# Recurrent layer of a fused four-layer kernel: row statistics on ScalarE, group scale and row mixing on GpSimd, single-term weights on TensorE

## The reference, cut to what matters

```
xa = ln(x) ; sx = shift(xa) - xa                      # shift: the row of the token before
xxx = tanh((xa + sx * maa_x) @ maa_w1)                # five low-rank rows
xm = xa + sx * (maa_stack + xxx @ maa_w2)             # five mixed inputs
w = exp(-exp(time_decay + tanh(xw @ td_w1) @ td_w2)) ; r, k, v = xr @ Wr.T, xk @ Wk.T, xv @ Wv.T
g = silu(xg @ Wg.T)
s = k v^T + w s ; out = r (u k v^T + s)               # a scan over 64 tokens, 32 heads of 8
og = (out - mean) / sqrt(var + 1e-5)                  # per head, 8 channels
x1 = x + (og * g) @ Wo.T
xc = ln(x1) ; sx2 = shift(xc) - xc
xk2 = xc + sx2 * ffn_maa_k ; xr2 = xc + sx2 * ffn_maa_r
out = x1 + sigmoid(xr2 @ Wfr.T) * (square(relu(xk2 @ Wfk.T)) @ Wfv.T)
```

## Time and profile before

| | us |
|---|---|
| median of 3 runs | 1036.51 (1035.86 to 1045.05) |
| the profiled execution, own time | 1037.27 |
| its span | 1035.4 |
| busy: PE | 946.3 (91%) |
| busy: DVE | 595.9 (58%) |
| busy: ACT | 431.0 (42%) |
| busy: POOL | 410.0 (40%) |

### The profile page before, as it was taken

The page is one execution under the profiler, slowest core; times in us unless marked ns, Lnnn a source line. Parts: engine busy times, 40 slices in busy tenths (PEclk is TensorE's granted clock), DMA queues, the critical chain, the costliest instruction groups (busy, mean ns, idle before and its releaser), DMA issues.

```text
span 1035.4 us, 21403 instructions
## 1 busy us (share of the span) xinstructions
PE 946.3 (91%) x8296; PEld 803.9 (78%) x8296; DVE 595.9 (58%) x1004; ACT 431.0 (42%) x910; POOL 410.0 (40%) x558
## 2 busy tenths in 40 slices
PE   6888887968989999999999999999996978999986
PEld 4667765856778888899887988888985877878854
DVE  5889993667644443334363444433357457988871
ACT  3566663237643333333343333333323223545542
POOL 2223253875366343333166432433317512333320
PEclk9999997999999999999998999999998998999997
DMA  9000000140011110111101111110100100000000
GB/s 307 11 2 1 3 1 11 42 150 1 2 52 47 51 51 24 47 36 51 47 19 54 37 51 46 51 51 21 41 16 22 41 1 1 1 6 7 6 12 15
DMA packets 24145, 37.12 MB, mean 36 GB/s; under 512 B 4432, under 2 KB 16528, under 8 KB 23824
## 3 DMA queue, kind: packets, MB, share of 16 engines
q1 hardware_dynamic: 24080, 36.23, 11.3%
HBM read 35.17 MB, written 1.05 MB: 35 GB/s over the span
## 4 chain that ended last, share of the span: by engine, by line
PE 76%; DVE 8%; ACT 7%; issue 4%; POOL 4%; DMA 1%; SPq 0%; ACTq 0%; POOLq 0%; DVEq 0%
PE ps L1193 16%; PE ps L722 11%; PE ps L1832 9%; PE ps L1210 9%; PE ps L1252 6%; PE ps L1228 3%; PE ps L811 3%; PE ps L394 2%; PE ps L345 2%; PE ps L1238 2%; PE ps L1983 1%; PE ps L1910 1%; PE ps L297 1%; ACT sb L1617 1%; PE ps L1871 1%
## 5 line engine op out<-in xcount | busy, mean ns | idle before, releaser
L772 POOL TENSOR_TENSOR sb<-sb 128x256 fp32r<-128x256 f32 (+1 forms) x128 | 95.5, 746 | 302.0 <-DMA sb<-in_heads_a 149.7
L1193 PE MATMUL ps<-sb 128*128 128x512 f32 x768 | 187.8, 396 | 1.0 <-issue 1.0
L1193 PEld LDWEIGHTS ps<-sb 128*128 128x128 f32 x768 | 139.6, 188 | 33.0 <-ACT sb L1318 3.2
L722 PE MATMUL ps<-sb 128*128 128x256 f32 x1152 | 148.7, 287 | 0.5 <-DVE sb L859 0.4
L722 PEld LDWEIGHTS ps<-sb 128*128 128x128 f32 x1152 | 142.5, 193 | 2.7 <-issue 0.8
L774 POOL TENSOR_TENSOR sb<-sb 128x256 fp32r<-128x256 f32 (+1 forms) x128 | 115.6, 903 | 10.0
L1832 PE MATMUL ps<-sb 128*128 128x128 f32 (+2 forms) x672 | 101.0, 309 | 12.4 <-ACT sb L2116 6.3
L1832 PEld LDWEIGHTS ps<-sb 128*128 128x128 f32 (+1 forms) x672 | 89.6, 202 | 21.8 <-issue 8.0
L1415 DVE SCALAR_TENSOR_TENSOR sb<-ps,sb 128x512 fp32r<-128x512 f32 x64 | 45.1, 747 | 97.5 <-ACT sb L1351 97.5
L1210 PE MATMUL ps<-sb 128*128 128x256 f32 x768 | 99.2, 285 | 0.4 <-DVE sb L1383 0.4
L1210 PEld LDWEIGHTS ps<-sb 128*128 128x128 f32 x768 | 95.0, 191 | 3.0 <-issue 0.9
(11 more groups left out here) (211 smaller groups left out, 1595.7 us busy)
## 6 DMA issues: line engine op xcount, KB each, us to landing
sb<-in_heads_a SPq DMA_DIRECT2D x32, 386.0 KB, 3.0
sb<-in_heads_c SPq DMA_DIRECT2D x16, 256.0 KB, 3.6
sb<-in_heads_b SPq DMA_DIRECT2D x32, 128.0 KB, 2.9
sb<-in_mlp_a SPq DMA_DIRECT2D x16, 128.5 KB, 2.1
sb<-in_mlp_b SPq DMA_DIRECT2D x16, 128.0 KB, 2.1
sb<-in_w_r SPq DMA_DIRECT2D x1, 2048.0 KB, 7.6
sb<-in_encT SPq DMA_DIRECT2D x1, 1024.0 KB, 5.9
sb<-in_ctx SPq DMA_DIRECT2D x1, 1024.0 KB, 8.3
```

The lines of the kernel that those rows point to most:

```text
L722: last = pe.matmul(m.acc(t), lhsT[x], rhs[w], start=opens and n == 0, stop=False, skip_group_check=True)
L772: pool.tensor_tensor(high, src, one, ALU.mult).then_inc(*G.did(name + "_high", u))
L1193: last = pe.matmul(m.ps[u][:, c, :], m.w_parts[u][w][:, (KD * q + k) * P:(KD * q + k + 1) * P], rows[x][:, k, c * 512:(c + 1) * 512], star ...
```

## The change

Five edits in the recurrent layer. (1) The statistics of both row norms leave DVE: ACT runs an Identity with a sum, a Copy that makes the negative mean, and a Square with a sum; POOL makes the variance, the power and the product of the two (three instructions where there were two). (2) DVE forms xa + sx * maa_x itself (`lora_rows`, two instructions per tile), and `lora` has one term. (3) POOL forms xk2 and xr2 (`ffn_rows`, five instructions on 128x256 per tile), and `ffn1` has one term. (4) The root and the reciprocal of the group norm go from ACT and DVE to POOL: one scale-and-add and one power of -0.5, both on 128x32. (5) The scaling of weights is gone except for one. Two edits of order in the first layer: DVE does `stats` and `variance` of the next item after `keys` in place of before it, and POOL does `row_split` first in its slot; and at its end TensorE does `turn_rows` of the last tile between the two first pieces of the MLP, with ACT doing `mlp_rows` ahead of the two Gelus.

```diff
@@ attn0, last slot: TensorE, ACT, DVE, POOL
                 fc1(pe, ph, m, 4, u, 0, 0)
-        turn_rows(slot - 3)
+                if u == 0:
+                    turn_rows(slot - 3)
+        if slot < SLOTS - 1:
+            turn_rows(slot - 3)
...
         rows(slot)
+        mlp_rows(slot - 3)
         if slot == SLOTS - 1:
             for u in range(STREAMS):
                 gelu_rows(act, ph, m, ACT.Gelu_apprx_tanh, u, 0, 0)
-        mlp_rows(slot - 3)
...
-        if slot:
-            stats(slot + 1)
-            variance(slot + 1)
         keys(slot)
         if slot == 0:
             vec.wait_ge(m.s_x[1], 16)
-            stats(1)
-            variance(1)
+        stats(slot + 1)
+        variance(slot + 1)
@@ rwkv_tensor
-                           [(m.maa_w1[:, k, cols], xa[:, k, :, 1:S + 1]) for k in range(KD)]
-                           + [(m.maa_w1s[:, k, cols], xa[:, k, :, 0:S]) for k in range(KD)])
+                           [(m.maa_w1[:, k, cols], m.xl[i % 2][:, k, :]) for k in range(KD)])
...
+            product(m.c1[:, e * P:(e + 1) * P], [(m.wr[:, W_FK, k, e * P:(e + 1) * P], m.xk[:, k, :]) for k in range(KD)])
+        product(m.c1[:, D:2 * D], [(m.xr[:, k, :], m.wr[:, W_FR, k, :]) for k in range(KD)])\
+            .then_inc(*done["kk_rr"].did(i))
@@ rwkv_scalar
+    def stats(i, tag, at, dst):
+        a, own = i % 2, m.own_act
+        total, squares, mean = m.mv[a][:, at, 0:1], m.mv[a][:, at, 1:2], m.rstd[a][:, at:at + 1]
+        if i >= 2:
+            act.wait_ge(*done[tag + "_turned"].at(i - 2))
+        act.activation(dst[a][:, :], m.x[:, i, :], ACT.Identity, accum_out=total).then_inc(*own.did(tag + "_sum", i))
+        act.wait_ge(*own.at(tag + "_sum", i))
+        act.activation(mean, total, ACT.Copy, scale=-1.0 / D).then_inc(*own.did(tag + "_mean", i))
+        act.wait_ge(*own.at(tag + "_mean", i))
+        act.activation(dst[a][:, :], m.x[:, i, :], ACT.Square, bias=mean, accum_out=squares)\
+            .then_inc(*done[tag + "_eps"].did(i))
...
         ffn_rows(slot - 5)
+        f_stats(slot - 4)
+        a_stats(slot + 1)
         rows(slot)
...
         square(slot - 3)
-        std(slot - 3)
@@ rwkv_vector
+    def lora_rows(i):
+        vec.wait_ge(*m.own_vec.at("sx", i))
...
+            last = vec.scalar_tensor_tensor(out=split(m.xl[i % 2][:, k, :]), in0=split(m.sx[i % 2][:, k * P:(k + 1) * P]),
+                                            scalar=m.col("maa_x", k), in1=m.xa[i % 2][:, k, :, 1:S + 1], op0=ALU.mult,
+                                            op1=ALU.add)
+        last.then_inc(*m.own_vec.did("xl", i))
@@ rwkv_gpsimd
+    def ffn_rows(i):
+        own, wide = m.own_pool, lambda name: bc(m.cols(name), 2, [P, KD, P])
+        tokens = lambda s: m.xc[:, :, :, s:s + S].rearrange("p k b s -> p (k b) s")
+        split = lambda x: x.rearrange("p k (b s) -> p (k b) s", b=2)
+        pool.wait_ge(*own.at("f_state", i))
+        pool.wait_ge(*done["xc"].at(i))
+        pool.tensor_tensor(split(m.xd), tokens(0), tokens(1), ALU.subtract).then_inc(*own.did("xd", i))
+        pool.wait_ge(*own.at("xd", i))
+        pool.tensor_tensor(m.xk, m.xd, wide("ffn_k"), ALU.mult)
+        pool.tensor_tensor(m.xr, m.xd, wide("ffn_r"), ALU.mult).then_inc(*own.did("xkr", i))
+        pool.wait_ge(*own.at("xkr", i))
+        pool.tensor_tensor(split(m.xk), split(m.xk), tokens(1), ALU.add)
+        pool.tensor_tensor(split(m.xr), split(m.xr), tokens(1), ALU.add).then_inc(*done["f_state"].did(i))
...
+    def group_rstd(i):
+        n = D // HS
+        pool.wait_ge(*done["gsum"].at(i))
+        pool.tensor_scalar(m.sm[0][:, :], m.sm[0][:, :], 1.0 / HS, EPS, ALU.mult, ALU.add)\
+            .then_inc(*m.own_pool.did("group_var", i))
+        pool.wait_ge(*m.own_pool.at("group_var", i))
+        if i >= 1:
+            pool.wait_ge(*done["normed"].at(i - 1))
+        pool.tensor_tensor(m.rc[0][:, :], m.sm[0][:, :], m.col("pow").to_broadcast([P, n]), ALU.pow)\
+            .then_inc(*done["gstd"].did(i))
...
     for slot in range(TILE_SLOTS):
+        f_state(slot - 7)
+        ffn_rows(slot - 7)
         f_rstd(slot - 6)
         a_state(slot - 2)
-        a_rstd(slot)
+        a_rstd(slot - 1)
         first(slot - 4)
+        group_rstd(slot - 5)
         receive(slot - 4)
-        f_state(slot - 6)
         gated(slot - 5)
         bonus(slot - 3)
```

More of the change, by code:

```diff
@@ L702, in attn0_gpsimd @@
             rstd(0)
+        row_split(slot - 4)
         row_rstd(slot - 3)
@@ L1973, in ffn1 @@
     def ffn1(i):
-        pe.wait_ge(*done["xc"].at(i))
         pe.wait_ge(*done["f_state"].at(i))
-        parts = [(m.wr[:, W_FK, :, :], m.wr[:, W_FR, :, :], k, 1) for k in range(KD)]\
-            + [(m.wfks, m.wfrs, k, 0) for k in range(KD)]
         for e in range(KD):
[L1979 to L1982, removed]
-                last = pe.matmul(m.c1[b * S:(b + 1) * S, D:2 * D], m.xc[:, k, b, s:s + S], wr[:, k, :], start=n == 0,
-                                 stop=n == len(parts) - 1)
-        last.then_inc(*done["kk_rr"].did(i))
+            product(m.c1[:, e * P:(e + 1) * P], [(m.wr[:, W_FK, k, e * P:(e + 1) * P], m.xk[:, k, :]) for k in range(KD)])
+        product(m.c1[:, D:2 * D], [(m.xr[:, k, :], m.wr[:, W_FR, k, :]) for k in range(KD)])\
+            .then_inc(*done["kk_rr"].did(i))
     @of_tile
@@ L2079, in std @@
     @of_tile
-    def std(i):
-        act.wait_ge(*done["gsum"].at(i))
-        act.activation(m.sm[0][:, :], m.sm[0][:, :], ACT.Sqrt, bias=m.col("eps"), scale=1.0 / HS)\
-            .then_inc(*done["gstd"].did(i))
-    @of_tile
     def heads(i):
@@ L2194, in shift @@
             .then_inc(*m.own_vec.did("sx", i))
+    @of_tile
+    def lora_rows(i):
+        vec.wait_ge(*m.own_vec.at("sx", i))
+        if i >= 2:
+            vec.wait_ge(*done["lora"].at(i - 2))
+        for k in range(KD):
+            split = lambda x: x.rearrange("p (b s) -> p b s", b=2)
+            last = vec.scalar_tensor_tensor(out=split(m.xl[i % 2][:, k, :]), in0=split(m.sx[i % 2][:, k * P:(k + 1) * P]),
+                                            scalar=m.col("maa_x", k), in1=m.xa[i % 2][:, k, :, 1:S + 1], op0=ALU.mult,
+                                            op1=ALU.add)
+        last.then_inc(*m.own_vec.did("xl", i))
     @of_tile
@@ L2277, in group_sum @@
         vec.wait_ge(*done["square"].at(i))
+        if i >= 1:
+            vec.wait_ge(*done["gstd"].at(i - 1))
         vec.tensor_reduce(m.sm[0][:, :], m.sq[:, :].rearrange("p (h j) -> p h j", j=HS), AX, ALU.add)\
             .then_inc(*done["gsum"].did(i))
[L2281 to L2284 removed]
     @of_tile
@@ L2323, in rwkv_vector @@
         products0(slot - 5)
-        f_variance(slot - 7)
         bonus(slot - 6)
@@ L2330, in rwkv_vector @@
         shift(slot - 3)
+        lora_rows(slot - 3)
         scan0(slot - 5)
-        group_rstd(slot - 6)
         group_norm(slot - 6)
@@ L2342, in rwkv_vector @@
         attended(slot - 6)
-        a_variance(slot)
-        f_stats(slot - 6)
         close(slot - 8)
@@ L2352, in rstd @@
     def rstd(i, tag, at):
+        a, own = i % 2, m.own_pool
+        var, squares, mean, scale = (m.mv[a][:, at, 0:1], m.mv[a][:, at, 1:2], m.rstd[a][:, at:at + 1],
+                                     m.rstd2[a][:, at:at + 1])
         pool.wait_ge(*done[tag + "_eps"].at(i))
-        norm_scales(pool, m, i % 2, at, (tag + "_pow", i), done[tag + "_rstd"].did(i))
+        pool.tensor_scalar(var, squares, 1.0 / D, EPS, ALU.mult, ALU.add).then_inc(*own.did(tag + "_var", i))
+        pool.wait_ge(*own.at(tag + "_var", i))
+        pool.tensor_tensor(scale, var, m.col("pow"), ALU.pow).then_inc(*own.did(tag + "_pow", i))
+        pool.wait_ge(*own.at(tag + "_pow", i))
+        pool.tensor_tensor(mean, mean, scale, ALU.mult).then_inc(*done[tag + "_rstd"].did(i))
     @of_tile
```

68 lines of the change are left out of this document (19 added, 49 removed).

## The result

The changed kernel takes 1071.03 us (median of 4 runs, 1068.21 to 1073.27) against 1037.92 (4 runs, 1035.86 to 1045.05): ratio 1.0305, 95% interval 1.0247 to 1.0363. The forecast was 1041, with a range to 1056; the change is 33 us slower. The profiled execution took 1072.52 us, its span is 1070.7.

What follows compares the result with a forecast made beforehand. The prediction saw TensorE setting the recurrent layer's pace, DVE close behind, and a loop of both bounding the first layer. 1037.3 + 11.7 (recurrent) - 7 (first layer) = 1042 profiled, so 1041 as median; 8-in-10 range 1022 to 1056.

Steps and rivals of the forecast that it cites:

- The line through three widths: Power on POOL: 550, 1034 and 1655 ns at 1, 4 and 8 columns, extended to 5.45 us at 32.
- DVE's wait: Recurrent layer's steady slots: DVE idles 3.2 us ahead of `group_norm` for POOL's power, which 2.7 us of work covers in part.
- rival (b): Power on POOL cheap at 32 columns, near a plain add's 0.73 us; TensorE sets 17.2 per slot; 1012; chance 0.12.
- -7 forecast: First layer: earlier `keys` save 5 us and the last tile's earlier rows 2.1; together -7, bounds 0 and -9.
- I take 20.5 per steady slot: Recurrent layer: a steady slot goes from 20.08 to 20.5 us, between 19.9 and 21.5.
- 0.6 for TensorE's clock behind it: Steady slots: after TensorE idles for `group_norm`, some 4 us at half speed push `mixes` about 0.6 us past DVE.
- the scans themselves do not seem to be stretched: DVE's scans in the recurrent layer: not lengthened by POOL's instructions, an argument against the shared-port rival of 1051.
- Rival (a): Slots 3 to 7: POOL's power takes the shared port, the second `lora_rows` waits; +10 us, 1051; with its like 0.30.
- My -3.5 for slots 0 to 2: Recurrent layer's first slots, without group norm: one-term `lora` and an earlier third end save 3.5 us, late start included.
- +9.2 forecast: Drain of the recurrent layer: uncovered powers of +3.1 in two slots, +3.9 at the last tile, -0.9 for the rest.
- -0.9 together: Drain: twice +3.7 of mixing, less about 2.5 of TensorE and a table load in two or three places each.
- hidden in the steady slots: POOL's five mixing instructions, 3.7 us with two waits: hidden in a steady slot, not in the drain.

Runs made afterwards that it cites:

- run 1: Changed kernel with the group norm's root put back as a square root on ACT and a reciprocal on DVE: 1042.21 us, ratio 1.0007.
- run 2: Kernel before with only the group norm's scale-and-add and power on POOL, replacing root and reciprocal: 1071.55 us, ratio 1.0287.
- run 4: Kernel before with only the new order of the first layer: 1035.0 us, ratio 0.9938.
- run 3: Changed kernel with the power on one column of the 32 only: 1040.33 us, ratio 1.0018.
- Run 5: On run 1, DVE's `ffn` moved from behind the five scans of `scan1` to ahead of the last three: 1033.18 us, ratio 0.9936.
- run 6: On run 1, POOL's mixing taken out and `ffn1` with two terms again: 1031.62 us, ratio 0.9893.
- run 7: On run 1, the edits of Run 5 and run 6 together: 1037.58 us, ratio 0.9974.

## Why the prediction was wrong, point by point

**Right: the price of the power, and its wait.** The line through three widths gave 5.45 us; it took 5.51 in the steady slots. DVE's wait was forecast at 3.2 and is 3.29. `lora_rows` takes 0.61 (forecast 0.6). The gap between my forecast and rival (b), 1041 to 1012, was 29 us; the power costs 31 (run 1) or 30 (run 2). The two halves of it hold as well, by the traces: 15.9 forecast for the five slots (+6.0 with it, -9.9 in rival (b)) and 14.8 found (112.87 in place of run 1's 98.05), 13.2 forecast for the drain and 16.2 found (86.1 in place of 69.9).

**Right: the first layer.** -7 forecast, -6.4 timed (run 4), with the interval from -4 to -9. The wait for `scores` went from 10.1 us to 3.7. The trace of the changed kernel has the gain where it arises, 6.4 us at 177.30.

**Wrong: everything else in the recurrent layer, by some 25 us.** Without the power the forecast has the kernel at 1012, a gain of 24.4, of which 17.4 in the recurrent layer. Runs 1 and 3 put it at 0.7 and 1.9 us above the kernel before: the first layer's 6.4 came, and the recurrent layer lost 7 or 8 where I had it gain 17.4.

The step that failed first is "I take 20.5 per steady slot": I put the slot together from DVE's own work and one wait, 16.7 + 3.2, and 0.6 for TensorE's clock behind it. The slots from tile 4 on are 26.2, 22.0 and 23.6. In the one of 22.0 the wait is right, 3.29. DVE's own work is 17.5 in place of 16.7, since the scans take 1.1 more and the multiply of `receive` 0.3 less, and its wait for `mixes` is 1.17 in place of 0.6. The one of 26.2 holds 5.7 of the 12.1 us by which the five slots together missed the forecast, and it is the one with the clock at 0.74. The terms that were missing or too small:

*The loop through `ffn`.* I let TensorE's shorter products come straight off the slot. They bring TensorE sooner to `turn_ffn`, which waits for an instruction that DVE has behind five scans. TensorE then idles there and DVE idles for `mixes`. Run 5 against run 1: 2.8 us a slot, 7 us in all. Did the trace before show the loop? `ffn` starts at 943.02, 0.51 us after its turn came. But `turn_ffn` comes later still, behind `ffn2` and `lora`; the chain of waits has it at

```profile
945.79 0.37 PE ps L1969 x2
```

so TensorE could lose a good 2 us more before it would stand for `ffn`. My estimate of the loop from these rows is 13.8 us on DVE to the end of `ffn` without its wait, and 3.4 for `turn_ffn`, `attended` and `mixes`: 17.2, the slot that rival (b) has. The order alone would have cost next to nothing. It came to 20.4 in run 1 because the scans took 1.0 more (5.12 for 4.16), the two TensorE steps 1.6 more at the lower clock, and DVE's part ahead of the scans 0.6 more.

*The scans and POOL.* I wrote that "the scans themselves do not seem to be stretched". The earlier trace rows said otherwise: three scans in 1.85 us, 0.62 each, and five in 4.16, 0.83 each. The first of the five took 1.83 us there, since POOL's multiply on 128x768 was in it. In the changed kernel `gated` and `bonus` meet the scans too, and the five take 5.25. The power is not needed for that: without it, in run 1, they take 5.12, since the shorter `ffn1` brings `turn_heads` forward. Rival (a) named the place wrongly (the second `lora_rows` ran beside the power and took its 0.3 us) but the kind rightly. It gave 1051.

*The entry.* My -3.5 for slots 0 to 2 had the late start inside. The trace has +3.8 from the last add of the MLP to tile 0 and -2.6 from there to tile 2, so +1.2. `lora` waits 2.56 us for the rows that DVE now makes, and its 12 matmuls and those of `mixes` run at a lower clock (0.72 from 830 to 844, where it was 1.00): 3.12 us where 24 took 3.07, and 2.93 in place of 1.60. Part of the 3.8 is not this layer's: run 4, which has only the first layer's order, takes 12.5 us there in place of 10.9, at a clock of 0.87.

*The drain.* +9.2 forecast, +20.0 found. 3 of the 10.8 us missing are the power: its three waits are 4.7, 4.7 and 5.8 us. The other 8 remain with the root put back: the drain of run 1 takes 69.9 us, 3.8 more than before, where rival (b) had 4 less. The two waits for the mixing, 7.1 us together, were in the sum as 7.4. Against them I had set about 8 us of TensorE's savings and of table loads, to come to -0.9 together. They did not show: TensorE had fewer instructions (254 in place of 354) and was busy for 50.17 us against 51.81, at a clock of 0.69 where it was 0.89.

*POOL's mixing* was hidden in the steady slots, as forecast: TensorE waits for it twice, both times in the drain. Yet mixing and one-term `ffn1` together cost 12 us (run 6), where I had booked them as a gain of TensorE. How these divide between the scans, the loop and the clock I can't tell; the edits of runs 5 and 6 do not add up (run 7).

## What to carry to other kernels

Work taken off the engine that sets the pace is worth only what the next loop leaves: before counting a saving, look for the instruction that it makes wait, and where that instruction stands in the other engine's queue. Price a POOL operation at its own width, and ask what else stands behind it in POOL's queue and which DVE instructions it will then meet. When one instruction runs in groups, divide each group's time by its count: two values for one form are a sign that another engine holds some of them up already. And look at the clock of each slot: a saving that leaves TensorE idle can be lost again in the matmuls behind.
